# Features of linear attention as a maximum: cap and constant on two tiles at once in SBUF, the product read from PSUM once

## What is computed

```
x2  = x1 + layernorm(expert outputs)                 # residual of the block before
qkv = layernorm(x2) @ W_qkv + b_qkv                  # 256 -> 768
q   = elu(q * 16 ** -0.5) + (1 + 1e-4)
k   = elu(k) + (1 + 1e-4)
```

## Time and profile before

| | |
|---|---|
| Runs | 3443.32, 3452.65 and 3454.3 us, median 3452.65 |
| Profiled execution | 3451.12 us, its span 3449.4 us |
| The phase of the change | about 1856 to 2141 us of the span |
| Granted TensorE clock over the span | 0.891 |
| Blocks in the phase | 16; steps with all three stages: 14 |

### The profile page before, as it was taken

The page is one execution under the profiler, slowest core; times in us unless marked ns, Lnnn a source line. Parts: engine busy times, 40 slices in busy tenths (PEclk is TensorE's granted clock), DMA queues, the critical chain, the costliest instruction groups (busy, mean ns, idle before and its releaser), DMA issues. The chain is left out here.

```text
span 3449.4 us, 59493 instructions
## 1 busy us (share of the span) xinstructions
PE 2928.8 (85%) x19969; PEld 2092.0 (61%) x19969; DVE 2259.5 (66%) x6090; ACT 1606.3 (47%) x2364; POOL 725.1 (21%) x854
## 2 busy tenths in 40 slices
PE   6768999999999477499673775999489999999998
PEld 5654444444444266399442664556278888888887
DVE  5548999999998288591223885344366666666665
ACT  2323767777777345244001553455334444444443
POOL 0011122222212133234674221222100000000000
PEclk9886999999999677599655998899789999999999
DMA  6776555665562388733675886655424242424241
GB/s 175 222 213 86 97 91 83 96 95 87 92 94 50 114 282 276 260 128 122 161 159 140 256 279 221 193 155 162 140 62 122 68 117 62 121 63 120 62 104 44
DMA packets 413439, 472.12 MB, mean 137 GB/s; under 512 B 91728, under 2 KB 300656, under 8 KB 412016
## 3 DMA queue, kind: packets, MB, share of 16 engines
q1 hardware_dynamic: 401408, 445.35, 50.0%
q0 software_dynamic: 10240, 14.16, 2.4%
q10 hardware_dynamic: 1648, 10.81, 0.9%
HBM read 271.95 MB, written 197.71 MB: 136 GB/s over the span
## 5 line engine op out<-in xcount | busy, mean ns | idle before, releaser
L529 ACT ACTIVATE att_pr<-att_e_ps 128x1024 f32<-128x1024 f32 (+2 forms) x640 | 567.2, 938 | 204.1 <-PE att_e_ps L581 204.0
L557 PE MATMUL att_m_ps<-att_ks,att_qs 63*128 63x512 f32 (+3 forms) x1536 | 466.1, 433 | 40.9 <-PEq L39 32.3
L491 DVE CUSTOM_DVE_ANT_0 att_kept<-att_m_ps,att_causal 128x256 f32<-128x256 f32 (+3 forms) x1024 | 448.5, 488 | 49.4 <-DVEq L39 21.9
L557 PEld LDWEIGHTS att_m_ps<-att_ks,att_qs 63*128 63x128 f32 x1536 | 234.6, 189 | 371.4 <-DVE att_mx L494 148.3
L494 DVE TENSOR_REDUCE att_mx<-att_m_ps 128x1 f32<-128x512 f32 x512 | 323.4, 684 | 21.5 <-PE att_m_ps L557 17.4
L601 PE MATMUL att_o_ps<-att_pr,att_vs 128*32 128x512 f32 (+3 forms) x3072 | 329.3, 502 | 3.4 <-issue 1.7
L470 POOL TENSOR_SCALAR_AFFINE_SELECT att_pr<-att_pr 128x256 f32<-128x256 f32 (+1 forms) x384 | 181.3, 484 | 698.6 <-PEq L572 695.0
L2566 ACT ACTIVATE fin_hh<-fin_hid 128x512 fp32r<-128x512 f32 x192 | 121.4, 632 | 415.4 <-DVE fin_hid L2412 302.1
L581 PE MATMUL att_e_ps<-att_qs,att_ks 64*128 64x512 f32 (+3 forms) x1536 | 269.3, 377 | 5.7 <-PEq L39 2.9
L2305 POOL TENSOR_TENSOR fin_rs<-fin_ve,fin_mhalf 128x4 f32<-128x4 f32 x48 | 48.3, 1007 | 941.3 <-POOLq L39 941.3
L2408 DVE TENSOR_TENSOR fin_hid<-fin_gate,fin_u_ps 128x512 f32<-128x512 f32 x192 | 131.6, 685 | 149.2 <-ACT fin_gate L2560 83.0
(11 more groups left out here) (317 smaller groups left out, 7040.2 us busy)
## 6 DMA issues: line engine op xcount, KB each, us to landing
fin_raw<-weights SPq DMA_DIRECT2D x32, 1024.0 KB, 12.6
att_qs<-q_high SPq DMA_DIRECT2D x128, 128.0 KB, 4.6
att_ks<-k_high SPq DMA_DIRECT2D x128, 128.0 KB, 6.0
attended<-att_ot SPq DMA_DIRECT2D x64, 256.0 KB, 2.0
exp_w<-w SPq DMA_DIRECT2D x128, 128.0 KB, 2.9
lqk_a<-acc SPq DMA_DIRECT2D x32, 512.0 KB, 6.2
attended<-lin_ot SPq DMA_DIRECT2D x32, 512.0 KB, 3.6
fin_x<-x SPq DMA_DIRECT2D x32, 512.0 KB, 4.7
```

The lines of the kernel that those rows point to most:

```text
L491: e.tensor_tensor_reduce(kept[:, n % MBUF, 0:w], m_ps[:, n % MBUF, 0:w], causal[:, BLK - w:], 1.0, -3e38, ALU.add, ALU.max, mx[:, h, at, q ...
L529: e.activation(out, src, ACT.Exp).then_inc(exp_done, 1)
L557: e.matmul(m_ps[:, (2 * i + n) % MBUF, 0:w], qs[rows, j, p, q * P:(q + 1) * P], ks[rows, j, p, h * BLK:h * BLK + w], start=True, stop=True ...
```

## The change

The feature is now taken as `max(min(exp(z), 1) + FE, z + 1 + FE)`, which is the same function. On DVE one instruction per two tiles caps the exponentials and adds FE, in place in SBUF, with two constants. Then one instruction per tile adds the shifted bias to the product in PSUM and takes the maximum with the capped tile. The tile `re` goes, and the bias tile holds the bias plus 1 + FE in place of the bias plus FE. A pair of tiles now waits for both its exponentials, and `step` puts a wait on DVE's own result between the capping and the first maximum.

```
-                        begun = []
-                        for k in range(5):
-                            if k < 4:
-                                e.wait_ge(exp_ready, k + 1)
-                                begun.append(step.begin(e.tensor_scalar(re[:, k], qk[:, k], bqke[:, k:k + 1], FE,
-                                                                        ALU.add, ALU.max)))
-                            if k:
-                                step.done(begun[k - 1])
-                                e.scalar_tensor_tensor(phi[:, j, k - 1], ex[:, k - 1], 1.0, re[:, k - 1], ALU.min,
-                                                       ALU.add).then_inc(phi_done, 1)
+                        for half in (slice(0, 2), slice(2, 4)):
+                            e.wait_ge(exp_ready, half.stop)
+                            step(e.tensor_scalar(ex[:, half], ex[:, half], 1.0, FE, ALU.min, ALU.add))
+                            for k in range(half.start, half.stop):
+                                e.scalar_tensor_tensor(phi[:, j, k], qk[:, k], bqk1[:, k:k + 1], ex[:, k], ALU.add,
+                                                       ALU.max).then_inc(phi_done, 1)
```

and, in the set-up of the phase:

```
-                step(e.tensor_scalar(bqke[:], bqk[:], FE, None, ALU.add))
+                step(e.tensor_scalar(bqk1[:], bqk[:], 1.0 + FE, None, ALU.add))
```

More of the change, by code:

```diff
@@ L1524, in phase_linear_qkv @@
         bqk = ph.sb("bqk", [P, 4])
-        bqke = ph.sb("bqke", [P, 4])
+        bqk1 = ph.sb("bqk1", [P, 4])
         bv = ph.sb("bv", [P, C])
@@ L1542, in phase_linear_qkv @@
         ex = ph.sb("ex", [P, 4, BLK])
-        re = ph.sb("re", [P, 4, BLK])
         phi = ph.sb("phi", [P, 2, 4, BLK])
```

## The result

| | Before | After |
|---|---|---|
| Runs, median (range) | 3453.48 (3443.32 to 3454.37, 4 runs) | 3418.59 (3416.13 to 3420.25, 4 runs) |
| Span of the profiled execution | 3449.4 | 3418.5 |
| Granted clock over the span | 0.891 | 0.892 |
| The phase of the change | 284.6 | 271.7 |
| of it, the 13 full steps | 199.18 | 190.15 |

The ratio is 0.9905, with an interval of 0.9885 to 0.9925: 35 us faster, where 13 were forecast from this median (11 from the profiled execution). 3440 was too high, and 3418.59 lies outside the range of 3431 to 3456. Of the 30.9 us between the two spans, 12.9 lie in the phase of the change (from POOL's first write to `vo` to the next phase's first instruction on POOL), 14.1 in the last phase, which the prediction had not looked at, and 3.9 in the others.

What follows compares the result with a forecast made beforehand. DVE was taken to set the pace of the stage's steps. Instructions 6.7 us, plus 5.3 of residual-add stretch, minus 1.0 of late loads, gave 11.0 less than 3451.12: 3440 us, range 3431 to 3456.

Steps and rivals of the forecast that it cites:

- The rest of the kernel is left as it is: Outside the changed stage: the prediction examined only that stage and gave the other phases no term.
- the remaining edits cost nothing: Bias instruction, freed tile `re`, SP and POOL issue, and PE's key transposes were taken to add no time.
- the stretch: Residual add L1674 lengthened by POOL's add at the shared port: 10.8 us in 13 steps, about half, 5.3, forecast to go.
- Carrying the distances through: Applying 13.7 us steps to 12 measured residual-add-to-POOL-add distances: all 10.8 us of stretch go, 1.5 of late loads come.
- rival 3: Capping on DVE runs at one element a cycle: features take 5.04 us, nothing saved, 3451 us; chance 0.14.
- The order of waits: DVE features: second capping waits for the fourth exponential, starting at 2.17 us; values wait for PE, at 4.35, not 5.05.
- The gain of the instructions alone: Features on DVE: 13 steps x 0.70 = 9.1 us, less 2.4 for late products, gives 6.7 us.
- late products: PE value products ending 4.7 us or more after the features start, in 4 of 14 steps: 4 x 0.6 = 2.4 lost.
- rival 2: Transfers set the pace: loads land 15.6 us after the residual add, steps take 14.8, 3444 us; chance 0.1.
- rival 1: POOL's add still falls on the residual add as often as before: gain 6.7 us only, 3444 us; chance 0.2.
- rival 4: Residual add L1674 collides worse with POOL's add, up to 2.0 us each: 6 to 10 us slower, 3459 us; chance 0.06.
- second place: The capping itself may contend with POOL at the shared interface, but only with an add of the filling steps; no size given.

Runs made afterwards that it cites:

- e1: The changed kernel with 16 satisfied waits (8 instructions) added to DVE's program at the start of the last phase: 3427.82 us, ratio 0.994.
- e4: The changed kernel with the capping on one tile at a time, four tensor_scalar of 128x512 in place of two of 128x1024: 3434.78 us, ratio 0.9966.
- e5: The changed kernel with POOL's add of a0 and a1 waiting until DVE has finished the residual add of the same step: 3414.92 us, ratio 0.9901.
- e6: The changed kernel with POOL's add waiting for a PE signal that the instruction ahead of DVE's residual add is done: 3406.75 us, ratio 0.9886.
- e9: The changed kernel run once more without any edit: 3414.88 us, ratio 0.9904 against the kernel before.
- e10: The changed kernel with 8 satisfied waits (4 instructions) added to DVE's program at the start of the last phase: 3420.29 us, one run.
- e7: The kernel before, with POOL's add waiting for a PE signal that the instruction ahead of DVE's residual add is done: 3433.31 us, ratio 0.9951.
- e2: The kernel before with 96 satisfied waits (48 instructions) added to DVE's program at the start of the last phase: 3437.13 us, ratio 0.9973.
- e8: The kernel before with 48 satisfied waits (24 instructions) added to DVE's program at the start of the last phase: 3438.77 us, one run.
- e11: The kernel before with 16 satisfied waits (8 instructions) added to DVE's program at the start of the last phase: 3444.48 us, one run.
- e12: The kernel before with 32 satisfied waits (16 instructions) added to DVE's program at the start of the last phase: 3437.78 us, one run.
- e13: The kernel before with 512 satisfied waits (256 instructions) added to DVE's program at the start of the last phase: 3462.12 us, one run.

## Why the prediction was wrong, step by step

**What failed first: the kernel outside the stage.** "The rest of the kernel is left as it is" and "the remaining edits cost nothing" were the steps. The code was as it was, but DVE's program was 8 instructions shorter ahead of a loop of the last phase, and this cut five stops there from some 4.9 us to 2.4, which nothing waits for. With the new features the last phase takes 997.9 and 996.6 with the long stops (e1, e4) and 984.3 to 987.3 without (after, e5, e6, e9, e10), with the old 998.4 (before, e7) and 983.0 to 986.0 (e2, e8, e11, e12): these 13 us follow the place alone. By the ratios, e1 against the change says 12 (0.994 and 0.9905 of 3450; their intervals overlap a little), e2 against the kernel before 9 (0.9973; 4 to 14 by its interval). No term of the sum stood for it, and no view of the changed stage could have shown it; the row of five waits on "issue", 115 us apart, stood in the profile of before.

**What was mis-sized: the stretch.** "I keep about half of the stretch: 5.3 gained." The executions with the old features and POOL's add unordered had 10.8, 10.4, 9.9, 13.3, 11.8 and 12.0 us of it in 13 steps, mean 11.4; with the new ones 9.8, 0.0, 2.4 and 0.0, mean 3.1. So 8.3 us, three quarters, go on the mean, with 5.3 forecast; all goes in two of the four, and 1.0 us in the first. Carrying the distances through had given all of it. No one number was right here: half was too little for three executions and too much for the first. The reasoning for the half, that a stretched step shifts the next, does hold where collisions go on: in the first execution six residual adds of the first eight steps were stretched, and from the ninth on all five steps were 13.7. There are two ways to run on, colliding or not. In the four executions of the change none fell back into collisions, and its step of 13.7 is shorter than the 14.4 from a residual add to POOL's next add; but e4, with a step of 13.8, did fall back, after a wait for late value products. That the second way always stays with the change is not shown.

**Where luck came in.** In the pair of executions of the result the phase is 12.9 us shorter, close to the 11.0 forecast, but not by the forecast's terms: the stretch gave 1.0 in place of 5.3, the filling steps 1.1 and the end of the phase, behind the last residual add, 2.9 (26.9 us at a granted clock of 0.82, 24.0 at 0.93), for neither of which the sum had a term.

**What held.** The capping at the fast rate (694 ns; rival 3 is refuted, and e4's 418 ns for 512 elements, with 694 for 1024, gives 0.54 ns an element). The order of waits: 2.18 and 4.36 us. The step: 13.69. DVE as the engine that sets the pace. The gain of the instructions alone: forecast 6.7 with four late products, 9.1 without; 7.8 by e6 and e7. (A maximum follows the other after 0.66 us, the upper end of what was allowed, not 0.63; the waits hide it.) That the second to start at the shared port waits, which e6 turned to use. DVE's waits in the 13 steps after, by releaser, have the value products, as foreseen, and the exponentials:

```profile
DVE lqk_nmr L734 <- POOL lqk_rs L1649: 12.8, 13, 1.0
DVE lqk_vo L1694 <- PE lqk_vp L716: 2.0, 3, 1.1
DVE lqk_ex L1689 <- ACT lqk_ex L1716: 0.5, 2, 0.3
```

**The rivals.** Transfers as the pace (rival 2) are refuted: e1 and e6 run eleven steps of 13.69 in a row, at 298 GB/s over the 13, and only their first two steps are longer (14.2 to 14.5). Collisions as now (rival 1) is what the first execution did (9.8 of 10.8 us), and what e1, e9 and e10 did not. The worse collisions (rival 4) did not come (its price with late loads is 3451 + 10 = 3461 by its own terms, not 3459). Its second place did, once: a capping in a filling step, with POOL's add begun ahead of it (timelines of POOL and DVE, after):

```profile
1893.16 2.39 POOL L1641 TENSOR_TENSOR lqk_a<-lqk_a 128x1024 f32<-128x1024 f32 x1 [1.46 <-POOLq L39]
...
1894.30 1.80 DVE L1689 TENSOR_SCALAR lqk_ex<-lqk_ex 128x1024 f32<-128x1024 f32 x1 [0.31 <-ACT lqk_ex L1716]
```

1.80 us in place of 0.69, over at 1896.10, 0.55 after POOL's add ends at 1895.55. The Trainium skill's rule ("SBUF — State Buffer", section "Who interferes with whom") that a `tensor_scalar` of the fast kind contends with GpSimd too agrees with it. It costs 1.1 us once.

**The sum, by the profiles.** The phase: 284.1 us on the mean of six executions with the old features (POOL unordered), 264.0 of four with the new, 20.1 less. Of it 7.8 are instructions and 8.3 collisions; 4 remain, of which 1 is in the filling steps (27.0 to 27.2 us in place of 28.0 to 28.6), 1 in the 13 steps, and 2 lie behind the last residual add, where the time goes with the granted clock and not with the features: 26.9 us at 0.82 (before), 25.6 at 0.87 (e2), 24.0 at 0.93 (after), 22.6 to 22.7 at 1.00 (e9 and, with the old features, e11). The last phase: 998 to 985, 13. Together 33 of the 35 of the medians. The 3.9 us of the other phases in the first pair belong to no cause shown; these phases differ from execution to execution (the first phase ends anywhere from 244.9 to 251.7 us, and the linear attention takes 310.0 to 319.5). Nor is it settled why the runs of one kernel spread by 19 us (before, 3437.18 to 3455.88).

## What to carry to other kernels

Compare all phases of the two traces, not only the one that was changed: an edit that alters the length of an engine's program moves every loop behind it, and a row of equal waits on "issue" at a loop's branch back is time that a few padding instructions may recover. Such a stop can also stand under the name of a wait for an engine that had long been done, so look at when the input was really ready. Where two engines meet at a port, let the one off the path wait: signal it from the instruction just ahead of the critical one, not from its end. And where a step is nearly as long as the distance to the event that disturbs it, expect different outcomes of the same program (190.15 and 181.67 us here), and take more than one profile before a cause is priced.

## What the runs showed of the hardware

- At the branch back of DVE's loop of 298 instructions it is 0.60 us from the last subtraction to the next product when the loop lies at +8, +16, +24 or +48; 2.97 to 3.31 at -8, -5 and -4; 5.26 to 5.84 at 0 and +256.
- The first 2.4 us of this stop cost the phase nothing here (984 to 987 us with it, 983 to 986 without); the further 2.3 to 2.8 cost it 13 us for five.
- The profile put the stop of 2.3 us down to a PE product, when the product needed had ended 5.00 us before (after, 2738.05).
- POOL's add of 128x1024, 2.35 us alone, takes 2.99 to 3.08 when it starts 0.4 to 0.5 us after DVE's residual add; in e6 it ends 3.47 us after the start of the residual add in step after step, whether it took 2.60 or 2.99. The other way round the residual add takes up to 3.33 in place of 1.21. A `tensor_scalar` of 128x4 (L728) that begins 0.45 us before the add's end takes 0.47 in place of 0.17 (e5).
- A `tensor_scalar` in SBUF of 128x1024 with two constants takes 694 ns, of 128x512 418; a maximum with one input from PSUM, one from SBUF and a bias per partition takes 746 ns for 128x512, as one with an input from PSUM alone, and follows its neighbour at 0.66 to 0.67 us.
- A wait that is already satisfied holds DVE for some 50 ns: 29.3 us with 512 of them (e13), 8.1 with 96 (e2), which is 21.2 us for 416.
